# Moving one copy, the normalisations, a chain of gate operations and two weight loads in a hand-written order of work

## The reference, cut to what matters

```python
xn = _layernorm(x, axis=-1)                     # x: (4, 4096, 1024)
s = _L0_attn_ref(xn, Wq, Wk, Wv, Wo, bo, Wg, bg, decay_param)   # gated linear recurrence, M = 64
g = _silu(_L0_ffn_ref(xn, w_gate, w_up, w_down))                # h = silu(xn Wg') * (xn Wu'); h Wd', hidden 3072
return x + s * g
```

## Time and profile before

| | us |
|---|---|
| median of the runs, 3 runs | 533.13 (532.1 to 556.47) |
| the profiled execution | 533.95 |
| span of its slowest core, 6 | 532.4 |
| spans of cores 0 to 5 and 7 | 525.3, 527.6, 529.2, 524.3, 525.8, 529.7, 530.4 |
| PE busy on core 6 | 506.7 (95%) |
| DVE, ACT, POOL busy | 361.6, 188.4, 121.3 |

### The profile page before, as it was taken

One profiled execution on the slowest core, in us unless ns is written; L12 is line 12 of the kernel. 1 busy time (PEld: TensorE's weight loads), 2 busy tenths in 40 slices (PEclk: granted clock), 3 DMA queues, 4 the chain that ended last, 5 costly groups with the idle time before them and its releaser, 6 DMA issues.

```text
span 532.4 us, 8803 instructions; the slowest of 8 cores (524.3 to 532.4 us)
## 1 busy us (share of the span) xinstructions
PE 506.7 (95%) x2722; PEld 239.8 (45%) x2722; DVE 361.6 (68%) x683; ACT 188.4 (35%) x296; POOL 121.3 (23%) x189
## 2 busy tenths in 40 slices
PE   4799989999999999989997999999999999999996
PEld 2455544445554444434553444444444444444442
DVE  4758667666777779887574567666666668967444
ACT  2524444554443311147311344333333333112111
POOL 2637312222327000335321531111111100000000
PEclk9999999999999999998999899999999999999999
DMA  7999999999999440377668995554454500042442
GB/s 219 217 106 158 162 166 154 136 153 139 159 159 197 69 159 22 114 223 212 184 116 202 174 185 88 89 86 77 75 91 76 84 9 0 1 134 85 119 138 79
DMA packets 37452, 66.77 MB, mean 125 GB/s; under 512 B 3295, under 2 KB 12639, under 8 KB 37408
## 3 DMA queue, kind: packets, MB, share of 16 engines
q0 software_dynamic: 18672, 36.19, 45.7%
q1 hardware_dynamic: 15504, 28.32, 17.1%
q10 hardware_dynamic: 3232, 1.72, 1.3%
HBM read 89.28 MB, written 8.39 MB: 183 GB/s over the span
## 4 chain that ended last, share of the span: by engine, by line
PE 86%; DMA 4%; DVE 3%; issue 2%; SPq 1%; ACT 1%; POOL 1%; DVEq 0%; ACTq 0%; POOLq 0%
PE bank L474 53%; PE bank L530 24%; DMA hT<-gu 2%; DMA xs<-xtm 2%; PE bank L655 1%; PE bank L542 1%; SPq L1344 1%; PE bank L466 1%; ACT xnt_all L1142 1%; PE bank L636 1%; PE bank L618 1%; PE bank L456 1%; DVE bst L860 1%; DMA out<-xr 1%; DVE bst L861 1%
## 5 line engine op out<-in xcount | busy, mean ns | idle before, releaser
L474 PE MATMUL bank<-xs,S_w 128*128 128x512 f16 x552 | 140.4, 381 | 1.4 <-ACT bank L1183 1.4
L474 PE MATMUL bank<-xnT,gu 128*128 128x512 f16 x368 | 94.9, 381 | 0.0
L474 PEld LDWEIGHTS bank<-xs,S_w 128*128 128x128 f16 x552 | 52.1, 98 | 62.3 <-issue 3.2
L1224 POOL DMA_DIRECT2D gu<-wgu x48 | 26.2, 545 | 201.7 <-PE bank L474 174.8
L1057 DVE TENSOR_TENSOR bank<-bank,m 128x512 f32<-128x512 f32 x46 | 32.2, 699 | 50.6 <-PE bank L474 50.6
L474 PEld LDWEIGHTS bank<-xnT,gu 128*128 128x128 f16 x368 | 34.7, 98 | 40.4 <-issue 1.5
L742 DVE SCALAR_TENSOR_TENSOR hT<-bank,sg_all 128x512 f16<-128x512 f32 x69 | 47.1, 689 | 7.2 <-PE bank L474 6.1
L1065 DVE TENSOR_TENSOR m<-bank,m 128x512 f32<-128x512 f32 x46 | 31.8, 690 | 26.7 <-PE bank L474 25.8
L474 PE MATMUL bank<-xs,gu 128*128 128x512 f16 x184 | 47.7, 382 | 0.0
L474 PE MATMUL bank<-xnT,S_w 128*128 128x512 f16 x184 | 47.7, 382 | 0.0
L530 PE MATMUL bank<-wd,hT 128*128 128x512 f16 x192 | 44.1, 379 | 0.0
(11 more groups left out here) (158 smaller groups left out, 722.5 us busy)
## 6 DMA issues: line engine op xcount, KB each, us to landing
gu<-wgu POOLq DMA_DIRECT2D x96, 256.0 KB, 7.9
xr<-xtm SPq DMA_DIRECT2D x16, 512.0 KB, 5.5
out<-xr SPq DMA_DIRECT2D x32, 256.0 KB, 2.2
xs<-xtm SPq DMA_DIRECT2D x12, 512.0 KB, 4.9
wd<-wdt POOLq DMA_DIRECT2D x24, 256.0 KB, 11.0
xr<-xpfm POOLq DMA_DIRECT2D x8, 512.0 KB, 12.6
hT<-gu SPq DMA_DIRECT2D x5, 512.0 KB, 10.8
wd<-xtm SPq DMA_DIRECT2D x4, 512.0 KB, 16.1
```

The costliest lines, as they stand in the source:

```text
L474: mm = pe.matmul(out=out[:], lhsT=weight(d), rhs=moving(d), start=(start and d == 0), stop=(d == 3), skip_group_check=True)
L1224: g.dma_start(out=gu[idx % NGU][:, 0:1024], in_=wgu[idx % NHC][:, 0:1024]).then_inc(ld_gate[idx % NGU], 16)
```

## The change

Four places of the order change, in the first half alone:

- `tcopy` 2 stands directly behind product (2,4) instead of behind the store and the two residual loads of that step.
- `norm` 9 to 15 are passed to `down_stage` by themselves and stand right behind `dp`, ahead of that product's evictions. `norm` 9 was the last step of k = 9 and becomes the first of k = 10; `norm` 10 to 15 stay at k = 11 to 16.
- `gates_0` moves from slot 7 to slot 8, `gates_1` from slot 9 to slot 10.
- `gu_pre` 24 and 25 move from `hooks[20]` to `hooks[22]`.

No instruction is added or removed and no wait is changed.

```diff
-def down_stage(half, hooks):
+def down_stage(half, hooks, norms):
...
         out.append(("dp", (P, m)))
+        out += norms.get(k, [])
         behind = []
...
         else:
             out += [("tcopy_act", 0)] if P == 0 else []
+            out += [("tcopy", 2)] if P == 2 else []
             out += [("dsilu", (P, 3)), ("dfin", (P, 3))] + sums(4) + tail(3)
             if P < 7:
                 behind += [("res_load", 2 * P + 2), ("res_load", 2 * P + 3)]
-            if P in (1, 2):
-                behind += [("tcopy", P)]
+            if P == 1:
+                behind += [("tcopy", 1)]
         out += hooks.get(k, []) + behind
...
-    slots[7] = [("gates_0", 0)]
-    slots[9] = [("gates_1", 0)]
+    slots[8] = [("gates_0", 0)]
+    slots[10] = [("gates_1", 0)]
...
-    for j in range(8):
-        hook(8 + j if j < 2 else 9 + j).append(("norm", 8 + j))
+    norms = {9 + j: [("norm", 8 + j)] for j in range(1, 8)}
+    hook(8).append(("norm", 8))
...
-    hook(20).extend([("gu_pre", 24), ("gu_pre", 25)])
+    hook(22).extend([("gu_pre", 24), ("gu_pre", 25)])
...
-    order += down_stage(0, hooks)
+    order += down_stage(0, hooks, norms)
...
-    order += down_stage(1, {})
+    order += down_stage(1, {}, {})
```

## The result

| | before | after |
|---|---|---|
| median of the runs (5 each), us | 532.13 | 527.96 |
| lowest, us | 531.47 | 526.06 |
| the profiled execution, us | 533.95 | 528.42 |
| span of core 6, the slowest in both profiles | 532.4 | 526.9 |
| mean of the spans of the 8 cores | 528.1 | 523.8 |

The ratio is 0.991, 95% interval 0.988 to 0.994: the changed kernel is faster by 0.9%, within the 2% of "no clear change", and 4.2 us by the medians, 4.8 us by the ratio, where 7.1 were forecast. (Executions in which the cores of one die ran longer than those of the other at a lower granted clock, or which lie over 1.5% above the fastest, as one of the kernel before with 556.47 us, are left out of every ratio.) Lines of `kernel.py` are two higher after the change: L474 is L476, L618 is L620, L1142 is L1144, L1344 is L1346.

A forecast was written before the change was run, and what follows sets the result against it. PE, busy for 95% of the span, bounds the kernel, with its stops and clock falls behind them. Core 6: 532.4 - 5.2 - 2.0 = 525.2; profiled 526.8, median 526.0. Range 522.5 to 530.

The forecast's parts named there:

- The copy: Behind product (2,4): `tcopy` 2 lands by 279 to 283.5, ahead of 287.2, so PE's 3.35 us wait goes.
- The term of 5.2 us for core 6: At product (3,4): PE's 3.35 us wait goes, and 1.8 us more come back if the clock stays up.
- The wait put down for the queue behind it: Residual loads on SP, held up 6 us by the copy issues, have some 10 us of cover; priced at nothing.
- The hand sum: `tr` 10 to `tr` 15: normalisations leave 2.0 us on core 6, 0.3 us where the clock had not fallen.
- the waits named: Behind moved normalisations: 0.35 us for `dfin` (1,1), then 0.2, 0.3 and 1.0 us at the following transposes.
- `norm` 15 ends by 253.6, in time: Chunk 15: `stats` 15 stays near 249.55 because its load's issue does not move; `tr` 15 starts about 254.3.
- The gates: POOL's `px_load` 2 issues 2.9 us earlier into a full queue: gain nothing, bounds 1.4 us gain, 0.9 us loss.
- The weights: `gu_pre` 24 and 25: POOL has no code for the steps between, so its queue is unchanged; no effect.
- The rule of the skill: Transfers from different engines share 16 DMA engines and interleave, so the moved copies would delay weights 24 and 25.
- a rival: Copies push back weights 24 and 25 before `win` 48: slower than before, 534 at 10.8 us of delay; chance 0.04.
- The sum: Core 6 span: 532.4 less 5.2 (copy) and 2.0 (normalisations) gives 525.2; median 526.0, faster by 7.1 us or 1.3%.
- Only the copy pays: Normalisations' waits come back in full, or the clock falls behind one of them: 528; chance 0.2.

The follow-up runs named there:

- the px load put ahead: Kernel before with the third px load ahead of slot 7's weight loads on POOL's queue, gates untouched: median 539.48 us against 540.68, ratio 0.998 without an interval.
- Done for real: Changed kernel with `gu_pre` 24 waiting for product (3,5) instead of (2,7), so weights 24 and 25 load two products later: 0.9844 to the kernel before.
- the first batch: Four runs together against the kernel before, same chip: copy alone 0.9913, normalisations alone 0.997, gates alone 1.0012, everything but the gates 0.9888.

## Why the prediction was right or wrong

The time lies in the range and the mechanism is as forecast; the size is 4.2 us by the medians (4.8 by the ratio) instead of 7.1. By its steps:

- **The copy.** Landing forecast between 279 and 283.5, measured 275.6. With the engines free it took 8.0 us instead of the bound of 12.3. The term of 5.2 us for core 6 holds for that core: in the run with the copy alone `tr` 15 to `win` 48 takes 33.99 us there, 5.1 less than before. But it was 4.5 to 4.9 on the four other cores whose clock had fallen, and 3.1 to 3.7 on the three whose clock had not (core 3: forecast 2.8). The mean of the eight cores is 4.0, and the run of it alone gained 4.6. The wait put down for the queue behind it (residual loads, `dres`) came: POOL waits 4.61 us for `xr<-xtm` and ACT got its results in time. Priced at nothing, and it cost nothing.
- **The normalisations.** The hand sum was 2.0 us where the clock had fallen before and 0.3 where it had not. Measured 1.91 on core 7 and 0.21 on core 0, but a mean of only 0.6 over the eight cores. That 1.91 is so near 2.0 is partly luck. Of the waits named, `dfin` (1,1) cost 0.7 (forecast 0.35) and `tr` 13 0.5 (0.3), but the longest, 1.0 us at `tr` 14, came on no core, and the rest went in gaps too short to be listed. The step that failed is the sentence "`norm` 15 ends by 253.6, in time". It held `stats` 15 near 249.55, 4.5 us behind the issue of its load at 245.03, since the issue would not move. The issue hardly moved (244.20, with this stage of the core 1.1 us earlier), but the landing did: 5.9 us on core 6 instead of 3.6, and there the part lost 0.14 us plus 1.7 us of clock instead of giving 2.0; on cores 1, 3 and 5 the landing at 4.2 to 4.3 us cost 0.4 to 0.5 us. Why it took 5.9 us there is open. This was known from no single row: the earlier trace rows shows `stats` 15 at 249.55 with DVE busy until then, which hides how late the load may come.
- **The gates.** Priced at nothing with bounds of -1.4 and +0.9 us; measured +0.6 us with an interval of -0.1 to +1.4. The argument, a full queue in which an earlier issue lands no earlier, holds, and the px load put ahead shows what would have shortened the wait.
- **The weights.** They have no effect, as forecast: only POOL has code for `gu_pre`, and POOL has none for the steps in between, so its order is the same with and without that edit. Done for real it gives nothing either.
- **The rule of the skill.** That transfers of different engines share the 16 DMA engines (the Trainium skill, "DMA: Bandwidth & Descriptors", "Issuing engines are not separate DMA queues") agrees with the slow landings before, 10.8 us. It made the weights a rival, by delay of either side. Neither came: the copies landed after 3.6/4.8/6.6 us with the weights issued 3.1 us behind the first of them and after 3.6/4.8/6.5 us with 7 us, and DVE did not wait for the weights in the changed kernel.
- **The sum.** It was made for core 6 alone: 532.4 to 525.2. But core 6 was the slowest for reasons of one execution. By the marks the gain runs from 2.9 us on core 3 to 6.8 on core 7 with a mean of 4.6 (0.6 from the normalisations, 4.0 from the copy), and the time is the largest of eight cores, each with its own stops: a wait of 0 to 2.5 us at slot 12, a late chunk 15, a fall of the clock behind either. Three such things stood on core 6 before: the wait at slot 12 and a fall of the clock behind each of the two stops. After the change it still had two, and the means of the spans went from 528.1 to 523.8, 4.3 us. (Over the five executions of the changed kernel that mean is 523.1, over eleven of the kernel before in the first batch 528.3.) I took the loss of the worst core as the gain of the kernel.
- **The rival that came nearer.** "Only the copy pays", with a chance of 0.2, gave 528, and the measured median is 527.96. Its second condition, that the clock falls behind one of the normalisations' waits, is what core 6 shows. As a statement on all cores it is too strong: three of the eight kept 1.5 to 1.9 us of the normalisations, and without the gate part copy and normalisations together have 0.9888 against 0.9913 for the copy alone, though these intervals overlap.

## What to carry to other kernels

When a step is moved out of the way of a stop, the gain is what the next chain leaves of it: list the input, the load and the semaphore of each following item, and give the load more time than one trace shows: here it took 3.6 us in one execution and 5.9 in another. In an in-order queue that is never empty, move a transfer past other transfers, since issuing it earlier in the same place did nothing here; and check first whether the engine that issues it has anything at all between the old and the new place. For the time of the slowest of eight cores, sum the terms on several cores, those without the bad luck too.

## What the runs showed of the hardware that was not expected

- A stop of the same length lets the clock fall on some cores and not on others. Behind the 2.4 us at `tr` 10 it went to 0.66, as a mean over 5 us, on four of eight cores in the kernel before, and stayed at 1.00 on the other four; behind the 2.12 us at `tr` 15 it fell on core 6. Stops of 1.0 to 1.7 us at `tr` 15, on nine cores in three other runs, brought no fall: the stretch to `win` 48 was 34.0 us on eight of them as on cores without a stop, and 34.3 us on the ninth, where PE waited 0.2 us for DVE.
- The clock also sinks without any stop, to 0.81 over 10 us with PE busy all of it, on two or four cores of one die of one chip, while the other die stayed at 1.00. The slowest core was one of these where it happened.
- SP's issue of a copy took 0.6 to 1.3 us with the DMA engines free, and up to 5.1 us when residual and weight loads were under way before it.
